# The first mixing of a two-layer adaptive FFN kernel: three pairs by quarters ahead of the first product, and their transfers ahead of half a weight block

## The reference

```
W = weights[condition]
y = jnp.einsum('bct,bcd->bdt', x, W)
x12 = jnp.einsum('bsk,mk->bsm', y, w12) + b12
x1, x2 = jnp.split(x12, 2, axis=-1)
x = x + jnp.einsum('bsm,nm->bsn', silu(x1) * x2, w3) + b3
```

## Time and profile before

| | |
|---|---|
| median of 3 runs | 975.05 us (974.64 to 975.47) |
| the profiled execution's own time | 975.11 us |
| its span | 973.3 us |
| TensorE busy | 967.9 us (99%) |
| VectorE busy | 799.6 us (82%) |
| ScalarE busy | 406.1 us (42%) |
| GpSimd busy | 36.5 us (4%) |
| HBM over the span | 86 GB/s |

### The profile page before, as it was taken

How to read it: one execution, slowest core, us unless ns; L and a number is a source line. 1 busy time by engine, 2 the same in 40 slices (tenths; PEclk the granted TensorE clock), 3 DMA queues, 4 the chain that set the end, 5 groups by cost and what they waited for, 6 DMA issues and landing times.

```text
span 973.3 us, 13504 instructions
## 1 busy us (share of the span) xinstructions
PE 967.9 (99%) x5270; PEld 799.9 (82%) x5270; DVE 799.6 (82%) x645; ACT 406.1 (42%) x374; POOL 36.5 (4%) x63
## 2 busy tenths in 40 slices
PE   9999999999999999999999999999999999999998
PEld 8888888888888888888888888888888888888886
DVE  4877877998867897778787888789987879886987
ACT  6553553443345433332356444544333543423221
POOL 3500000000000000000110000000000000000001
PEclk9999999999999999999999999999999999999999
DMA  9032044024012101240541211521340131022013
GB/s 354 5 108 88 0 160 186 20 74 177 35 44 101 73 1 65 72 189 1 196 153 44 87 43 45 215 87 31 119 155 1 44 131 43 1 72 81 1 44 129
DMA packets 23341, 84.48 MB, mean 87 GB/s; under 512 B 2722, under 2 KB 6834, under 8 KB 17522
## 3 DMA queue, kind: packets, MB, share of 16 engines
q1 hardware_dynamic: 21024, 75.77, 21.5%
q0 software_dynamic: 2112, 7.36, 2.0%
q10 hardware_dynamic: 146, 0.52, 0.2%
HBM read 75.25 MB, written 8.39 MB: 86 GB/s over the span
## 4 chain that ended last, share of the span: by engine, by line
PE 98%; DMA 1%; SPq 0%; DVE 0%; issue 0%
PE banks L714 32%; PE banks L715 31%; PE banks L716 31%; PE banks L776 1%; DMA r<-x_pairs_in 1%; PE banks L830 1%; PE banks L795 1%; SPq L568 0%; PE banks L814 0%; PE banks L845 0%; PE banks L861 0%; DVE r L1172 0%; SPq L522 0%; SPq L599 0%; SPq L601 0%
## 5 line engine op out<-in xcount | busy, mean ns | idle before, releaser
L714 PE MATMUL banks<-s_hi,t_hi 128*128 128x512 f32 x1344 | 525.6, 391 | 0.0
L715 PE MATMUL banks<-s_lo,t_hi 128*128 128x512 f32 x1344 | 523.2, 389 | 0.0
L716 PE MATMUL banks<-s_hi,t_lo 128*128 128x512 f32 x1344 | 523.0, 389 | 0.0
L714 PEld LDWEIGHTS banks<-s_hi,t_hi 128*128 128x128 f32 x1344 | 252.3, 188 | 54.7 <-issue 1.0
L716 PEld LDWEIGHTS banks<-s_hi,t_lo 128*128 128x128 f32 x1344 | 252.3, 188 | 52.2
L715 PEld LDWEIGHTS banks<-s_lo,t_hi 128*128 128x128 f32 x1344 | 252.3, 188 | 51.7
L1039 DVE TENSOR_TENSOR t_lo<-w,t_hi 128x1024 fp32r<-128x1024 f32 x134 | 160.0, 1218 | 12.1 <-ACT t_hi L949 12.1
L1167 DVE TENSOR_TENSOR r<-banks,r 128x1024 f32<-128x1024 f32 x102 | 123.5, 1219 | 44.7 <-PE banks L716 41.5
L949 ACT CAST t_hi<-w 128x1024 fp32r<-128x1024 f32 x134 | 136.6, 1048 | 50.9 <-PE banks L716 42.2
L917 ACT CAST s_hi<-st 128x2048 fp32r<-128x2048 f32 x40 | 76.5, 1913 | 177.0 <-PE banks L716 122.6
L1039 DVE TENSOR_TENSOR s_lo<-st,s_hi 128x2048 fp32r<-128x2048 f32 x40 | 91.6, 2289 | 45.7 <-ACT s_hi L917 45.7
(11 more groups left out here) (90 smaller groups left out, 406.6 us busy)
## 6 DMA issues: line engine op xcount, KB each, us to landing
w<-w_up_in SPq DMA_DIRECT2D x15, 1024.0 KB, 4.8
w<-w_base_in SPq DMA_DIRECT2D x10, 1024.0 KB, 4.8
w<-w_down_in SPq DMA_DIRECT2D x8, 1024.0 KB, 5.2
r<-x_t_in SPq DMA_DIRECT2D x8, 1024.0 KB, 6.2
w<-w_lin_in SPq DMA_DIRECT2D x8, 1024.0 KB, 5.5
out_t<-r POOLq DMA_DIRECT2D x14, 512.0 KB, 3.3
st<-x_pairs_in SPq DMA_DIRECT2D x11, 512.0 KB, 5.7
we<-w_expin_in SPq DMA_DIRECT2D x10, 512.0 KB, 4.4
```

The costliest lines, as they stand in the source:

```text
L714: pe.matmul(out, w_hi, x_hi, start=start, stop=False, skip_group_check=True)
L715: pe.matmul(out, w_hi, x_lo, start=False, stop=False, skip_group_check=True)
L716: return pe.matmul(out, w_lo, x_hi, start=False, stop=stop, skip_group_check=True)
```

## The change

Four edits are made, all for the first half. Pairs 2 and 3 are mixed by quarters instead of whole, where they stood. Pair 6 is mixed, by quarters as before, ahead of the first product instead of within it; only pair 7 is left within it. SP issues pairs 5 and 6 ahead of the second half of the first weight block; pair 4 was there already. The banks of the pairs change so that each fits (`mix_bank`: pair 3 takes banks 0 and 1 behind pair 0, pair 4 banks 2 and 3 behind pair 1, pair 5 banks 6 and 7, pair 6 banks 4 and 5 behind pair 2), and with them the waits: the first product waits for the fourth and fifth copy of a pair instead of the first and second, and pair 3 waits for a copy, pair 5 for none. On ScalarE the copy of pair 3 moves ahead of the first weight cast, and the copy of pair 6 stands ahead of the activations of product 1. The quartered mixing becomes a function of its own.

```diff
-MIX_LATE = (6, 7)
+MIX_LATE = (7,)
+MIX_QUARTERS = (2, 3, 6, 7)
...
-    return ((0, 2, 4, 6, 4, 6, 4, 6) if h == 0 else (4, 6, 4, 6, 0, 2, 0, 2))[c]
+    return ((0, 2, 4, 0, 2, 6, 4, 6) if h == 0 else (4, 6, 4, 6, 0, 2, 0, 2))[c]
...
             sp.dma_start(w_half(0, 0), w_up0[0][:, 0:8 * P]).then_inc(w_first_loaded, 16)
-            load_x(0, 4)
+            for c in range(4, 7):
+                load_x(0, c)
             sp.dma_start(w_half(0, 1), w_up0[0][:, 8 * P:]).then_inc(w_loaded[0], 16)
-            for c in range(5, PAIRS):
+            for c in range(7, PAIRS):
                 load_x(0, c)
...
-                    pe.wait_ge(mixed_copied, (1, 7)[i] + g // 2)
+                    pe.wait_ge(mixed_copied, (4, 7)[i] + g // 2)
...
-                    if c >= 4:
-                        pe.wait_ge(mixed_copied, c - 1)
+                    if c in (3, 4, 6):
+                        pe.wait_ge(mixed_copied, {3: 1, 4: 2, 6: 3}[c])
+                    if by_quarters(0, c):
+                        mix_quarters(0, c, bank)
+                        continue
...
+            def mix_quarters(h, c, bank):
+
+                for k in range(K):
+                    for q in range(2):
+                        for j in range(2):
+                            rows, cols = slice(j * S, (j + 1) * S), slice(q * S, (q + 1) * S)
+                            last = pe.matmul(banks[cols, bank + j, k * S:(k + 1) * S],
+                                             x_pair(h, c)[rows, k * P + q * S:k * P + (q + 1) * S],
+                                             mix[rows, c, rows], start=True, stop=True, skip_group_check=True)
+                last.then_inc(mixed_full, 1)
...
             def mixing():
-                for c in range(3):
+                for c in range(4):
                     copy_mixed(0, c)
                 t_split(-1, 0, (0,))
-                copy_mixed(0, 3)
                 wait_block(act, 0, 0)
...
                 t_split(-1, 0, (1,))
-                copy_mixed(0, 4)
-                copy_mixed(0, 5)
+                for c in range(4, PAIRS - len(MIX_LATE)):
+                    copy_mixed(0, c)
```

More of the change, by code:

```diff
@@ L227, in dve_own @@
     return [dve_half(n, 0), []]
-MIX_LATE = (6, 7)
+MIX_LATE = (7,)
+MIX_QUARTERS = (2, 3, 6, 7)
 MIX_BETWEEN = {(2, 3): (0, 1), (3, 3): (2, 3), (5, 1): (4, 5), (6, 1): (6, 7)}
 def mix_bank(h, c):
-    return ((0, 2, 4, 6, 4, 6, 4, 6) if h == 0 else (4, 6, 4, 6, 0, 2, 0, 2))[c]
+    return ((0, 2, 4, 0, 2, 6, 4, 6) if h == 0 else (4, 6, 4, 6, 0, 2, 0, 2))[c]
 def by_quarters(h, c):
-    return h > 0 or c in MIX_LATE
+    return h > 0 or c in MIX_QUARTERS
 def dve_scales(n):
@@ L815, in mixing @@
                     last.then_inc(mixed_full, 1)
+            def mix_quarters(h, c, bank):
[7 more added lines that the diff above has]
+                last.then_inc(mixed_full, 1)
             def mixing_between(h, pairs):
                 for c in pairs:
-                    bank = mix_bank(h, c)
                     wait_mixing(h, c)
@@ L825, in mixing_between @@
                         wait_taken(pe, phase_of(h - 1, "expup", 1 if c < 4 else 4), 2 * (c % 2))
[L826 to L833, removed]
+                    mix_quarters(h, c, mix_bank(h, c))
             def route(n, g):
```

## The result

The changed kernel takes 978.10 us in the median of 12 runs (976.39 to 980.03), the kernel before 975.03 (974.64 to 975.47): a ratio of 1.0029, 95% interval 1.0021 to 1.0036. It is 3.1 us slower, clear of noise. The forecast was 975.7, in a range of 974.2 to 976.8: wrong. The runs are not scattered evenly: of 18 (these twelve and the six of the last experiment), six lie between 976.4 and 977.1, eleven between 977.9 and 978.7, one at 980.0, while the kernel before stays within 1 us. Something happens in some runs and not in others. Each run's mean granted clock says in large part what: it is 0.998 in 11 of the 12 longer runs, and 0.999 or 1.000 in all six shorter ones and in one longer one (978.72). The seven with the higher clock (they kept their clock, in short) have a median of 976.5, the eleven others one of 978.2.

A forecast was written before the change was run, and what follows sets the result against it. TensorE, busy 99% of the span, was taken as the bound, with VectorE's weights late at product 2: max(-0.67, +0.63) = +0.63, and 975.11 + 0.63 = 975.74 us, range 974.2 to 976.8.

The forecast's parts named there:

- Pair 4's start and the early stop: TensorE's mixing: pair 4 still starts at 13.22, waiting for its data, after standing still 1.7 us from 11.5.
- my 5.74: TensorE's mixing of pairs 0 to 3: two whole pairs at 1.81 us each, two quartered at 1.06 each.
- My restart lag of 0.25: TensorE restarting on a transfer: 0.25 us after landing (15.52 to 15.77), applied to pair 4's landing at 13.0.
- First product: TensorE: starts at 17.84 instead of 17.55, +0.29; product 2 reachable on TensorE alone at 41.04, a gain of 0.67.
- The half block's landing: Second half of the first weight block lands at 16.8 instead of 14.3, as the transfer whose place it takes.
- My own bound: Half block's latest landing: one transfer more, 16.8 + 1.25 = 18.05, costing +1.9 us.
- ScalarE's extra copy and the chain to product 2: ScalarE casts product 1's activations 1.52 us later, at 20.47; VectorE readies product 2's weights at 42.19; product 2 +0.63.
- The slack of 0.94: VectorE ahead of product 2: its first weights were split by 40.77, product 2 started at 41.71, leaving 0.94 us.
- The clock: TensorE: stops of 1.7 and 1.3 us might drop it to the low level, 976.6 or more; rows alone give 975.7.
- rival B: Clock falls during the 1.7 us stop ahead of pair 4, for about 4.3 us: +1.5, 976.6; chance 0.04.
- the 1.3 us ahead of product 2: TensorE waits about 1.3 us for VectorE's weight split; product 2 starts near 42.3, +0.63 carried to the end.

The follow-up runs named there:

- the last experiment: The changed kernel run once more without any change, for another profile and the spread: 978.17 us in six runs.
- quarters alone: The kernel before with pairs 2 and 3 mixed by quarters and nothing else changed: 975.87 us, ratio 1.0015.
- pair 6 copied later: The changed kernel with ScalarE's copy of pair 6 behind the activation cast of product 1 instead of ahead of it: 975.68 us, ratio 1.0008.
- whole pairs: The changed kernel with pairs 2, 3 and 6 mixed whole, only pair 7 by quarters: 976.93 us, ratio 1.0020.
- the version meant to beat both: The kernel before, pairs 5 and 6 issued ahead of the second half block, pair 5 also quartered, copies of pairs 4 and 5 behind product 1's activation cast: 974.54 us.
- the zeros in the stop's place: The changed kernel with five matmuls of zeros, about 2.2 us, ahead of TensorE's wait for product 2's operands: 976.94 us.
- transfers alone: The kernel before with pairs 5 and 6 issued ahead of the second half block, mixing and copies as before: 974.58 us, ratio 0.9996.
- half early: The changed kernel with the second half of the weight block issued behind pair 4 again, pairs 5 to 7 behind it: 976.11 us, ratio 1.0015.
- code alone: The kernel before with the change's transfer order, three of five warm-up matmuls replaced by 48 small ones, results unread: 975.75 us, ratio 1.0010.

## Why the prediction was wrong

- **Pair 4's start and the early stop**: forecast 13.22 and 1.7 us; measured 12.81 and 0.85. The first mixing started 0.17 later, the two whole and two quartered pairs took 0.29 more than my 5.74, and the transfer landed 0.4 earlier. Small. (My restart lag of 0.25 was a slip: the landing in rows 4 and 5 is 4.86 + 10.7 = 15.56, which makes it 0.21.)
- **First product**: forecast 17.84, measured 18.04; pair 6 waited for its late transfer (16.7, not 15.5). TensorE alone would have been at product 2 at 41.27 (its last matmul ahead of the stop starts at 41.04, and they stand 0.23 apart), forecast 41.04. Right in kind.
- **The half block's landing**, the term taken at 16.8: 17.93. This is the first step that failed. I took the landing of the transfer whose place it takes, and so took the bytes ahead of it for all that matters. (My own bound, 18.05 and +1.9, held it, but gives 977.0 and so stood outside the range of up to 976.8.) The quartered pairs, which I had priced on TensorE only, bring 80 more matmul instructions ahead of the first product (24 each for pairs 2 and 3, all 32 of pair 6), and with them a fetch of code comes at 13 to 15 us instead of 19. Quarters without the swap have the late landing, the swap without quarters does not, and idle code in the warm-up brings it back.
- **ScalarE's extra copy and the chain to product 2**: right, term by term: cast at 17.92, three copies, the activations at 21.59, the weights of product 2 at about 43.3. The slack of 0.94 was right too. With the landing at 17.9 the sum of the forecast gives +1.8; measured +1.75 and +1.58. Five of the seven runs that kept their clock lie at 976.4 to 976.6, inside the range.
- **The clock**: the step that cost the range. I had it as rival B, with 0.04, and at the wrong stop: after the 1.7 us ahead of pair 4, while I gave the 1.3 us ahead of product 2 no price. It fell at product 2, by the mean clock in 11 of 18 runs, and cost 1.68; with it the median is 978.1, without it the runs lie at 976.5. The falls behind 1.92 us in the quarters alone and in 3 of 9 runs behind 1.5 us say that a stop of 1.3 us was no safe one to leave without a price. The two failures hang together: with a stop of 1.0 us (pair 6 copied later) the clock stayed up in all eleven runs. The Trainium skill, "TensorE: Matmul & The Clock Gate", Part 1, has the slow level as the default that activity lifts; the trace agrees, at 43.46 and, in the quarters alone, at 16.63.
- **The chances**: a late landing and a falling clock were each in the text, but as separate ends. Their sum, 978.1, was outside a range in which either alone lay. Rival B's 976.6 lies near the lower group of runs by chance: those are the runs in which the clock did not fall.

What stays open: the pause of 0.6 to 1.04 us among the second half's small matmuls, in the profiles of the changed kernel (one of two), of pair 6 copied later and of whole pairs; the kernel before has none in its profile, and no run of it is more than 0.7 us above its median. In these three an instruction fetch begins 0.1 to 0.3 us behind the start of the stretch of small matmuls (at 498.5, stretch from 498.21, in the changed kernel). But in the version meant to beat both one begins 0.4 us behind it (494.1, stretch from 493.69) with no pause, so the fetch alone does not explain it, and no experiment moved the pause on purpose. Open too are what the run of 978.72 lost, why the fetch comes when it does (0 to 24 added instructions left it at 18 to 19.5 us, 45 to 80 brought it to 11.8 to 14.8, not in proportion), and what decides in a single run whether the clock falls.

## What to carry to other kernels

Price a moved or split operation on all engines down to the next product that is short of slack, and look at how much slack each has: here 0.94 us on VectorE, and everything beyond it was paid in full. Count the instructions of a rewrite as well as its time, since code is fetched over the same DMA engines as data; where small instructions stand close together in a stage that waits for transfers, the fetch shows. And a stop of TensorE has two prices, its length and the clock behind it, so a forecast in which a stop appears should hold both, and their sum.

## What the runs showed of the hardware

One fetch of some 16 KB of code (the queue's row counts 42 packets and 0.69 MB over the kernel before) made a 512 KB transfer land 1.4 to 1.7 us later than 1.25 us behind the one ahead of it:

| kernel | fetch begins, us | landing in order, us |
|---|---|---|
| before | 19.5 | pair 4 13.0, half 14.3, pair 5 15.6, pair 6 16.8 |
| transfers alone | 18.6 | pair 4 12.4, 5 13.7, 6 14.9, half 16.2 |
| whole pairs | 19.1 | pair 4 12.5, 5 13.9, 6 15.1, half 16.3 |
| changed | 14.0 | pair 4 12.6, 5 13.9, 6 **16.7**, half 17.9 |
| changed, again | 13.5 | pair 4 12.3, 5 13.6, 6 **16.3**, half 17.6 |
| pair 6 copied later | 14.8 | pair 4 12.6, 5 13.8, 6 15.1, half **17.9** |
| half early | 13.7 | pair 4 12.5, half 13.8, pair 5 **16.5**, 6 17.7 |
| quarters alone | 14.2 | pair 4 12.4, half 13.7, pair 5 **16.4**, 6 17.7 |
| code alone | 11.8 | pair 4 **13.9**, 5 15.2, 6 16.4, half 18.2 |

A landing up to 0.3 us behind the fetch's beginning is spared, the next one is late, and those behind it are late with it. The 1 MB block behind them all lands at 21.9 before and after (issued at 6.40 and 6.58); by then the kernel before has had its own fetch, at 19.5, so this does not say that the lateness is made up. The fetch's row has 6.4% of 16 engines over its microsecond, as much as one engine busy all through. The Trainium skill, "DMA: Bandwidth & Descriptors", "Queues, rings and completion order", says that a copy is split over the engines and that each engine takes turns between the queues that have work for it. By that, one engine held by a packet of code would hold up a landing that needs all of them; the row's size agrees, but no run shows it engine by engine, and the lateness is 0.4 to 0.7 us more than the 1.0 us that the packet takes.

The clock fell behind stops of TensorE of 1.92, 2.03, 2.19 and 3.02 us in the profiles, and not behind those of 0.80, 0.85, 1.02, 1.53 and 1.83. By each run's mean granted clock (0.998 or less where it fell), it fell in no run of the kernels with up to 1.02 us or with the zeros in the stop's place, in 3 of 9 with 1.53, in none of 11 with 1.83, in 4 of 11 with 1.92, in 11 of 18 with 2.03 and 2.19, and in 4 of 5 with 3.02; the stop's length is that of the profiled run. During each of the four stops the granted clock is still 1.00, and it falls to 0.50 only when TensorE is at work again: at 43.7 us in the changed kernel, 0.2 us behind the restart. At product 2 the fall cost 1.68 us each time, nine matmuls in 3.72 us.
